# A four-layer graph network on one core: the way into layer 1 prepared inside layer 0's attention

## The reference, cut to what matters

```
# layer 0
h = relu(layernorm(x));  u = (h@W)@a[:F];  v = (h@W)@a[F:]
e = leaky_relu(u + v.T, 0.2)                      # 2708 x 2708
A+ = softmax(where(adj>0,  e, -big));  A- = -softmax(where(adj>0, -e, -big))
x  = x + elu(concat(A+ @ h, A- @ h) @ wtrans)
# layer 1, 8 heads of 64 columns
h = relu(layernorm(x));  nX = heads(h @ W)
nX = a_ln * (nX - mean) / (std + eps) + b_ln
k  = leaky_relu(nX@a1 + (nX@a2).T) * adj,  masked where adj == 0
x  = x + elu(softmax(k) @ nX + nX)
```

## Time and profile before

| | us |
|---|---|
| median of 3 runs | 2699.87 (2698.82 to 2702.06) |
| profiled execution, its own time | 2702.05 |
| its span in the profile | 2700.1 |
| PE busy | 2484.8 (92%) |
| DVE busy | 1991.5 (74%) |
| ACT busy | 1729.1 (64%) |

### The profile page before, as it was taken

The page is one execution under the profiler, slowest core; times in us unless marked ns, Lnnn a source line. Parts: engine busy times, 40 slices in busy tenths (PEclk is TensorE's granted clock), DMA queues, the critical chain, the costliest instruction groups (busy, mean ns, idle before and its releaser), DMA issues. The chain is left out here.

```text
span 2700.1 us, 54411 instructions
## 1 busy us (share of the span) xinstructions
PE 2484.8 (92%) x20735; PEld 1537.6 (57%) x20735; DVE 1991.5 (74%) x3876; ACT 1729.1 (64%) x3162; POOL 40.5 (1%) x53
## 2 busy tenths in 40 slices
PE   7959999999999759999999995789989979999999
PEld 4524444444444339999999994334436735555554
DVE  5758999999997669999999986582246624455684
ACT  3438888888886558988888985851124544444542
POOL 1200000000000000000000000000000000000000
PEclk9979999999999879999999997999999989999999
DMA  4133334433331454111111114102211143434452
GB/s 179 33 113 124 129 138 143 156 129 129 132 120 72 168 179 177 40 39 41 39 29 39 39 28 176 71 23 68 81 52 40 39 133 96 117 109 130 125 141 52
DMA packets 186467, 261.02 MB, mean 97 GB/s; under 512 B 97161, under 2 KB 127689, under 8 KB 180485
## 3 DMA queue, kind: packets, MB, share of 16 engines
q1 hardware_dynamic: 180085, 229.25, 26.7%
q10 hardware_dynamic: 6160, 28.85, 3.3%
HBM read 198.45 MB, written 59.39 MB: 95 GB/s over the span
## 5 line engine op out<-in xcount | busy, mean ns | idle before, releaser
L1630 PE MATMUL m_acc<-m_y,m_b 128*128 128x260 f16 x3696 | 633.6, 275 | 21.9 <-DVE m_b L1416 20.5
L1633 PE MATMUL m_acc<-m_y,m_at 128*128 128x130 f16 x3696 | 630.4, 221 | 0.0
L1379 ACT ACTIVATE m_above<-m_u,m_nvs 128x512 bf16<-128x512 f32 (+1 forms) x864 | 519.6, 681 | 53.0 <-DVE m_b L1416 52.3
L1630 PEld LDWEIGHTS m_acc<-m_y,m_b 128*128 128x128 f16 x3696 | 359.6, 97 | 76.6 <-DMA m_at<-at 20.2
L986 PE MATMUL m_acc<-keep_z_hi,m_p_hi 128*128 128x512 f16 x968 | 362.1, 378 | 15.4 <-DVE m_p_lo L828 12.4
L1633 PEld LDWEIGHTS m_acc<-m_y,m_at 128*128 128x128 f16 x3696 | 363.8, 98 | 0.0
L989 PE MATMUL m_acc<-keep_z_lo,m_p_hi 128*128 128x512 f16 x924 | 349.9, 379 | 0.0
L991 PE MATMUL m_acc<-keep_z_hi,m_p_lo 128*128 128x512 f16 x924 | 348.7, 377 | 0.0
L1416 DVE TENSOR_TENSOR m_b<-m_above,m_at 128x1024 f16<-128x1024 bf16 (+1 forms) x432 | 278.1, 649 | 28.1 <-ACT m_above L1379 10.6
L722 ACT ACTIVATE m_p_hi<-m_pm 128x512 f16<-128x512 f32 x242 | 150.9, 623 | 88.0 <-DVE m_pm L820 81.0
L808 DVE TENSOR_TENSOR m_sc<-m_r,m_g_row 128x512 f32<-128x512 f32 x242 | 165.5, 684 | 21.4 <-DMA m_g_row<-part 17.2
(11 more groups left out here) (362 smaller groups left out, 5275.5 us busy)
## 6 DMA issues: line engine op xcount, KB each, us to landing
keep_a_rows<-adj ACTq DMA_DIRECT2D x40, 704.0 KB, 4.3
m_at<-adjT SPq DMA_DIRECT2D x11, 1408.0 KB, 8.5
at<-m_at SPq DMA_DIRECT2D x22, 704.0 KB, 3.9
keep_at_first<-at SPq DMA_DIRECT2D x22, 704.0 KB, 4.1
m_at<-adjT SPq DMA_DIRECT2D x11, 1280.0 KB
m_at<-at SPq DMA_DIRECT2D x5, 2816.0 KB, 16.8
m_u<-rows SPq DMA_DIRECT2D x40, 256.0 KB, 4.2
low<-m_lw SPq DMA_DIRECT2D x32, 256.0 KB, 5.4
```

The source lines that it names most:

```text
L1379: act.activation(pair(above, a % RA, nb)[:, i], u[:, g % RU, 0:nb], ACT.Relu, bias=nvs[:, k, 2 * p + i:2 * p + i + 1], scale=STEEP).then_i ...
L1630: pe.matmul(full.rearrange("p l y e -> p (l y e)"), pair(b01, (m // 2) % RB, nb)[:, m % 2, q // 2, half], y12[:, k % 2, j].rearrange("p l ...
L1633: last = pe.matmul(full[:, :, 1, :], at[:, i0 + q // 2, j, half], y2[:, k % 2, j], start=False, stop=(j == T - 2), skip_group_check=True)
```

## The change

In the last block of `attention0`, and only there, `convert` turns two tiles a unit in units 0 to 10 (tile j and tile j + 11) and none afterwards; SP then stores both halves, waits for the stores, and loads the two halves of layer 1's split weights into the places of `at16`. SP also loads the first two row tiles of x1 (256 rows) into the place of `a_rows`; DVE and ACT work out their layernorm between the units (`first_rows` at units 6, 7, 8, 10 and 11, one square root after unit 9, the two normalised rows after units 12 and 13). SP no longer waits at the end for the last store of x1; `prep1` does in front of the chunk that holds those rows. `a_rows` and `at16` move to the other end of the on-chip memory.

`prep1` no longer loads the weights nor tiles 0 and 1, skips their moments, root, shift and normalise, and transposes them from `x_first`. Its chunks are 2, 2, 6, 6 and 4 tiles. ACT writes the first head's 64 columns of each product to the kept tile `c` besides `c_out`, and issues four DMAs of one adjacency block each (`at_early`) at tiles 4, 6, 8 and 10. The layernorm's a and b are loaded, and b scaled, in `prep1`. `attention1` has blocks 0 to 3 and the first head's columns already, and loads only the rest; the second head's columns are loaded one DMA later.

```diff
...
                     load_x(max(ib - 1, 0)) if ib != 1 else None
+                    if not more:
+                        sp.wait_ge(am_made, 4 * ib + 3)
+                        sp.dma_start(x_first.rearrange("p (q d) -> p q d", q=2), x_blocks("x1")[0]).then_inc(x1_in, 16)
                     store_mask(ib, 0)
                     if more:
                         load_mask(ib + 1, 0)
                         spread(ib + 1)
+                    else:
+                        store_mask(ib, 1)
+                        for half in range(2):
+                            sp.wait_ge(at16_out[half], 16 * IB)
+                            sp.dma_start(keep["w1"][half], dram["w1s"][half]).then_inc(w1_in, 16)
                     if ib > 0:
                         store_x(ib - 1)
-                    store_mask(ib, 1)
                     if more:
+                        store_mask(ib, 1)
                         load_mask(ib + 1, 1)
                 load_x(IB - 1)
                 store_x(IB - 1)
-                sp.wait_ge(x_out, 16 * IB)
-                for half in range(2):
-                    sp.wait_ge(at16_out[half], 16 * IB)
...
                 def convert(m):
+                    if m < UNITS - T:
+                        convert_tile(m)
+                    elif m < UNITS - HJ:
+                        convert_tile(m)
+                        convert_tile(m + HJ)
+
+                def convert_tile(m):
                     ib, j = divmod(m, T)
...
+                    if ib == IB - 1 and j == 9:
+                        act.wait_ge(x1_link, 3)
+                        act.activation(sd1[:, 0], sd1[:, 0], ACT.Sqrt).then_inc(x1_root, 1)
+                    if ib == IB - 1 and j in (12, 13):
+                        act.wait_ge(x1_link, 5)
+                        q = j - 12
+                        act.activation(x_first[:, q * D:(q + 1) * D], x_first[:, q * D:(q + 1) * D], ACT.Relu, bias=sd1[:, 2, q:q + 1],
+                                       scale=sd1[:, 1, q:q + 1]).then_inc(x1_ready, 1)
                     if ib > 0 and j in O_AT:
...
+                def first_rows(j):
+
+                    if j == 6:
+                        dve.wait_ge(x1_in, 16)
+                        for q in range(2):
+                            last = dve.bn_stats(mv1[:, q, 0:6], x_first[:, q * D:(q + 1) * D])
+                        last.then_inc(x1_link, 1)
+                    if j == 7:
+                        dve.wait_ge(x1_link, 1)
+                        for q in range(2):
+                            last = dve.bn_aggr(mv1[:, q, 6:8], mv1[:, q, 0:6])
+                        last.then_inc(x1_link, 1)
+                    if j == 8:
+                        dve.wait_ge(x1_link, 2)
+                        dve.tensor_scalar(sd1[:, 0], mv1[:, :, 7], 1e-5, None, ALU.add).then_inc(x1_link, 1)
+                    if j == 10:
+                        dve.wait_ge(x1_root, 1)
+                        dve.reciprocal(sd1[:, 1], sd1[:, 0]).then_inc(x1_link, 1)
+                    if j == 11:
+                        dve.wait_ge(x1_link, 4)
+                        dve.scalar_tensor_tensor(sd1[:, 2], mv1[:, :, 6], -1.0, sd1[:, 1], ALU.mult, ALU.mult).then_inc(x1_link, 1)
...
+                    else:
+                        first_rows(j)
                 low(UNITS - 1)
+                dve.wait_ge(x1_ready, 2)
...
+        w_hi, w_lo = (part.rearrange("p (k n) -> p k n", n=NX) for part in keep["w1"])
+        w_in, x1_out = keep["w1_in"], keep["x1_out"]
+        kit.semaphores += [w_in, x1_out]
+        CH = [(2, 2), (4, 2), (6, 6), (12, 6), (18, 4)]
...
-                for c, (t0, n) in enumerate(CHUNKS):
-                    sp.dma_start(x_all[:, t0:t0 + n, :], x_t[:, t0:t0 + n, :]).then_inc(x_in[c], 16)
-                    if c == 0:
-                        for i, part in enumerate((w_hi, w_lo)):
-                            sp.dma_start(part[:].rearrange("p k n -> p (k n)"), dram["w1s"][i]).then_inc(w_in, 16)
-                        sp.dma_start(valid[:], dram["valid"]).then_inc(v_in, 16)
+                for ring in tuple(s.values()) + (h_ready,):
+                    sp.sem_inc(ring, 2)
+                for n_c, (t0, n) in enumerate(CH):
+                    if t0 + n == T:
+                        sp.wait_ge(x1_out, 16 * IB)
+                    sp.dma_start(x_all[:, t0:t0 + n, :], x_t[:, t0:t0 + n, :]).then_inc(x_in[n_c], 16)
+                sp.dma_start(valid[:], dram["valid"]).then_inc(v_in, 16)
+                sp.dma_start(keep["aln"][:], dram["aln"].broadcast_to([P, DH])).then_inc(ln_in, 16)
+                sp.dma_start(keep["bln"][:], dram["bln"].broadcast_to([P, DH])).then_inc(ln_in, 16)
...
+                sp.wait_ge(at_in, 16 * EARLY)
...
+                    if isinstance(t, int) and t < 2:
+                        return
...
+                    act.activation(c[:, 0, ds(t, 1), 0:DH].rearrange("p o d -> p (o d)"), main[:, b, 0:DH], ACT.Copy, scale=1 / WS).then_inc(c_copied, 1)
...
+                def root_of(t, b):
+                    if not (isinstance(t, int) and t < 2):
+                        root(act, t, b, std, s)
+
+                def load_at(i):
+                    act.dma_start(at_early[:, i], dram["at16"][i]).then_inc(at_in, 16)
+
                 act.sem_inc(tp_ready, 2)
-                pipeline(act, (2, high), (4, lambda t, b: root(act, t, b, std, s)), (3, normalise), (0, finish),
-                         before=[(8 + 2 * k, lambda k=k: weights_2(k)) for k in range(KC)])
+                pipeline(act, (2, high), (4, root_of), (3, normalise), (0, finish),
+                         before=[(8 + 2 * k, lambda k=k: weights_2(k)) for k in range(KC)] + [(4 + 2 * i, lambda i=i: load_at(i)) for i in range(EARLY)])
+                act.wait_ge(c_copied, T)
...
+                    of = keep["x_first"][:, t * D:(t + 1) * D] if isinstance(t, int) and t < 2 else h[:, b, :]
                     for k in range(KC):
-                        last = pe.transpose(tp[:, b, k, :], h[:, b, k * P:(k + 1) * P], keep["ident"][:])
+                        last = pe.transpose(tp[:, b, k, :], of[:, k * P:(k + 1) * P], keep["ident"][:])
...
-                here = lambda c: dve.wait_ge(x_in[c], 16)
-                pipeline(dve, (0, dots), (2, split), (5, lambda t, b: moments(dve, t, b, x_all, stats, mv, std, s, gate)),
-                         (4, lambda t, b: shift(dve, t, b, mv, std, rstd, nmr, h_ready, s, gate)), (0, sum_squares),
-                         before=[(t0 - 6, lambda c=c: here(c)) for c, (t0, n) in enumerate(CHUNKS)]
+                here = lambda n_c: dve.wait_ge(x_in[n_c], 16)
+
+                def moments_of(t, b):
+                    if not (isinstance(t, int) and t < 2):
+                        moments(dve, t, b, x_all, stats, mv, std, s, gate)
+
+                def shift_of(t, b):
+                    if not (isinstance(t, int) and t < 2):
+                        shift(dve, t, b, mv, std, rstd, nmr, h_ready, s, gate)
+
+                pipeline(dve, (0, dots), (2, split), (5, moments_of), (4, shift_of), (0, sum_squares),
+                         before=[(t0 - 6, lambda n_c=n_c: here(n_c)) for n_c, (t0, n) in enumerate(CH)]
...
+                dve.wait_ge(ln_in, 32)
+                then(dve.tensor_scalar(keep["bln"][:], keep["bln"][:], 2.0, -1.0, ALU.mult, ALU.add))
...
+        at_early, at_late = keep["at_early"], kit.sb("at_late", [IB - EARLY, T, BW], F16)
         u = kit.sb("u", [RU, 2, BW])
-        c = kit.sb("c", [2, T, YW])
+        c = keep["c"]
...
+        def at_of(i0, nb=1):
+
+            return at_early[:, i0:i0 + nb] if i0 < EARLY else at_late[:, i0 - EARLY:i0 - EARLY + nb]
...
-                load_c(0)
-                sp.dma_start(aln[:], dram["aln"].broadcast_to([P, DH])).then_inc(ln_in, 16)
-                sp.dma_start(bln[:], dram["bln"].broadcast_to([P, DH])).then_inc(ln_in, 16)
                 load_u(0)
+                for hf in range(2):
+                    sp.sem_inc(c_in[hf], 16)
                 for i, (i0, nb) in enumerate(BLOCKS):
-                    sp.dma_start(at[:, i0:i0 + nb], dram["at16"].rearrange("i p t c -> p i t c")[:, i0:i0 + nb]).then_inc(at_in[i], 16)
+                    if i0 < EARLY:
+                        sp.sem_inc(at_in[i], 16)
+                    else:
+                        sp.dma_start(at_of(i0, nb), dram["at16"].rearrange("i p t c -> p i t c")[:, i0:i0 + nb]).then_inc(at_in[i], 16)
                     if i < 2:
                         load_u(i + 1)
-                    if i == 1:
+                    if i == 2:
                         load_c(1)
...
-                dve.tensor_scalar(d2[:], d2[:], LS, None, ALU.mult)
-                dve.wait_ge(ln_in, 32)
-                dve.tensor_scalar(bln[:], bln[:], 2.0, -1.0, ALU.mult, ALU.add).then_inc(set_up, 1)
+                dve.tensor_scalar(d2[:], d2[:], LS, None, ALU.mult).then_inc(set_up, 1)
                 dve.wait_ge(set_up, 1)
```

(31 more changed lines are left out.)

17 lines of the change are left out of this document (9 added, 8 removed).

## The result

The changed kernel takes 2692.88 us (median of 9 runs, 2691.93 to 2694.19), the kernel before 2700.61 beside it (9 runs, 2698.82 to 2702.87): a ratio of 0.997, 95% interval 0.9961 to 0.9979, so 7.7 us less. Measured again later (after_again) it was 0.9973 (0.9963 to 0.9982). The forecast was 13.4 us less. The direction is right; the size is just outside the range.

A forecast was written before the change was run, and what follows sets the result against it. PE, the busiest engine, was taken to be idle mainly between attention0 and prep1 and at attention1's start. +4.1 - 12.0 + 0.4 - 5.9 = -13.4 us, giving 2686.5 us, range 2681.5 to 2692.5.

The forecast's parts named there:

- The last block: a wait is added: Attention0's last block: ACT's convert waits 5.5 us for the half's load, delaying PE's tile 1; +4.1 us.
- So the data ends at 815.0 ... It lands at 815.8.: Last block: bytes over the windows' rates end the half's data at 815.0; 0.8 us follow before it lands.
- My upper bound of 5.3: Last block: the +4.1 us delay becomes 5.3 if the small loads end 1.2 us later.
- The idle time lowers PE's clock: Rival, last block: PE's 4.1 us idle drops its clock, losing 2.2 us more, 2688.7 in all; chance 0.18.
- The end of attention0: Attention0's end into prep1: without SP's store wait and with tiles ready, first products come 12.0 us sooner; bounds -9 and -13.
- Inside prep1: Prep1: ACT's extra copy and b's scaling cost +0.4 us behind the last tile; adjacency loads zero, range 0 to 2.
- 2.8 + 4 stays at that bound: Prep1: a store of `c_out` beside a 4 us adjacency load still lands about within the 6.7 us of two tiles.
- The start of attention1: Attention1's start: DVE goes on 4.9 us sooner and the 1.2 us adjacency wait goes; -5.9 us, bounds -6.4 and -3.5.
- The table loads: Last block, unit 9: two table switches and a root take 2.8 us of ACT's lead, leaving 1.3, adding nothing.
- the slower rival: Rival, prep1: ACT's loops reload tables, nine turns x 2.6 = 23.4 us, giving 2709.9; chance 0.03.

The follow-up runs named there:

- late: Changed kernel, but last-block ACT converts one tile a unit in units 0 to 3, two in units 4 to 12; ratio 0.9943 to the kernel before.
- pairs_only: Kernel before, with only the two converts a unit in the last block's units 0 to 10; 2716.19 us, ratio 1.003 to the kernel before.
- fill: Changed kernel plus 24 extra matmuls while PE would wait for the last block's tile 1; ratio 0.9968 to the kernel before.
- early2: Changed kernel, with row tile 2 of the next stage also loaded in attention0's last block; ratio 0.9977 to the kernel before.
- land: Changed kernel, but SP waits for the last block's second half to land before issuing the x loads; ratio 0.9975 to the kernel before.
- late_wait: The one-convert-then-two kernel (late) with SP's wait for the store of x put back at attention0's end; ratio 0.9952 to the kernel before.
- best_c: late plus early2 with prep1's loads spread, on-chip copy of c made first, adjacency loads at tiles 6, 10, 14, 16; ratio 0.9925 to the kernel before.

## Why the prediction was wrong

**The step that failed is "The last block: a wait is added", the term +4.1.** Measured: +7.6, shown by late (gone with the stall) and by pairs_only (there with the stall alone). The stall is the one described; the term is off by 3.5 us in two parts, 1.4 us of idle time and 2.1 us of low clock.

- "So the data ends at 815.0 ... It lands at 815.8." ACT went on at 817.07, 1.3 later, and the whole chain with it (high at 818.59 for 817.3, PE at 820.07 for 818.8). The bytes were counted rightly, but dividing them by the mean rate gave the time at which nearly all had moved. The last pieces ended at 816.05, 1.05 us later, and ACT waits for these too. They had ended at 816.11 in the kernel before, so its trace showed this already. The rest is the time behind the last piece, 1.0 for my 0.8. The Trainium skill (DMA: Bandwidth & Descriptors, Anatomy of one DMA) fits, for DMAs that GpSimd issues, a fixed cost of about 2.0 us per transfer, most of it the receipt of the last write. SP's DMAs show 0.85 us from the issue to the first piece (808.34 to 809.19 in the kernel before) and 0.9 to 1.0 behind the last one, together about 1.8, near that figure. The 1 MB of x behind the half, the other candidate, accounts for 0.2 of ACT's wait. My upper bound of 5.3, "if the small loads end 1.2 us later", comes near the idle time alone (5.4); it leaves out the clock.
- "The idle time lowers PE's clock", the rival with 0.18 and a price of 2.2 us, is what happened: PE stood 5.45 us, the clock fell 3.1 us into the gap, and fill and early2 put 2.1 us on it. I had counted it as one case against the forecast, because the row I read it from has the fall 4.1 us behind the last work and I expected PE to stand 4.1. In the five profiles with the stall the clock fell 2.6 to 4.5 us into it (after_again 2.6, pairs_only 3.0, after 3.1, early2 4.1, land 4.5). Even a stall of the forecast length would have met the fall in three of them, so this belonged into the forecast itself.

**The end of attention0**: -11.3 for -12.0. The wait of SP is worth 2.0 as forecast (late_wait: 2.4). What falls short is the first load, 4.5 us for 3.5; the second chunk's wait no longer shows. Why the load takes longer stays open: in late_wait, where the last store has landed before it starts, it still takes 4.13.

**Inside prep1**: +0.8 for +0.4. What comes behind the last tile is +0.4 as forecast. The clock came back 3.8 us behind the first product instead of 4.9, and tile 0 takes 0.6 us less for it. Against it stand 1.8 us of ACT's waits for stores of c, of which 0.9 reach PE; I had taken them as zero with 2 as bound. "2.8 + 4 stays at that bound" overlooked two things. A store waits behind what SP has issued before (up to 9.6 us in early2), and beside an adjacency block in ACT's queue it takes up to 6.95 us, while the 6.7 us of two tiles leave it 6.0, because it is issued 0.8 after ACT's copy starts. In best_c all these waits are gone.

**The start of attention1**: -6.2 for -5.9. Right, and none of its bounds was needed: DVE waits for no DMA.

**The table loads** cost nothing on the path: they lie in unit 9, ACT's timeline of the kernel after:

```profile
839.78 1.28 ACT L802 ACT_TABLE_LOAD   x1
841.08 0.20 ACT L802 ACTIVATE m_sd<-m_sd 128x2 f32<-128x2 f32 x1
...
841.70 1.28 ACT L725 ACT_TABLE_LOAD   x1
842.99 0.51 ACT L725 ACTIVATE m_e<-m_sc,keep_v 128x256 f32<-128x256 f32 x1
```

1.28 us each and the next operation 0.01 to 0.02 us behind, as in the earlier trace rows. The Trainium skill (ScalarE: Activation LUTs, What ACT_TABLE_LOAD costs) has 1.38 us of drain in a switch besides the load; here the measurement decides, there is none, and no PE gap follows. Inside prep1's loops no table is loaded (its two loads, at 891.09 and 974.38, lie ahead of them and behind), so the slower rival did not happen.

What stays open: the profiles differ by 9.3 us, the medians by 7.7 and 7.0. The profile of before lies near the top of its runs (2702.05, runs to 2702.87), 1.4 us above their median; the rest is inside the interval.

## What to carry to other kernels

An early step that puts a wait on data still in flight is priced by the last piece and what follows it, not by the bytes and the mean rate; here that was 1.3 us. If the matmul engine would stand about as long as it takes its clock to fall in the traces (here 2.6 to 4.5 us), the low clock belongs into the same case, not into a rival beside it. Move such a step by a few units before giving it up: four units later the same converts cost 0.2 us or less, where they had taken 7.6 of 16.7 us gained. A gain at the head of a stage lasts only until the first resource that is booked by its loads: here stores beside and behind loads took back 4 us until the loads were spread.

## What the runs showed that I had not expected

- The granted clock was low for 6.8 us in each of the five profiles with the stall. What differs is how much of that lay on work, because it began earlier or later in the idle time: 3.1 us in after_again, 3.5 in pairs_only, 4.4 in after, 4.6 in early2, 5.1 in land. The time from tile 1 to the end of the block follows it (59.5, 59.6, 60.1, 60.2, 60.4).
- Keeping the clock up across the idle stretch between two stages gained nothing (90.9 against 91.0 us from the first load to the end of prep1).
- A load of 1280 KB followed by three of 20 KB was usable 7.96 or 7.97 us after the first issue in five profiles and 7.79 in land. Its last piece ended 6.9 to 7.0 us after that issue in all of them.
